# The sweep's convolution as two column tiles of 64 output rows, with the padding columns left out

## The chip, the cores and the metric

One NeuronCore of one Trainium2 chip, one launch. The metric is the device time of the launch in microseconds (us), the median of several runs. All data are float32.

## What is computed

The input x has shape (4, 64, 128, 128): 4 images, 64 channels, 128 rows, 128 columns. Four blocks follow each other, each as x = x + block(groupnorm(x)). Blocks 1 and 4 are pointwise networks over the 64 channels (block 4 with an attention over 8 heads). Blocks 2 and 3, each with four directional sweeps, hold the change. Cut to what matters, one sweep is

```python
def sweep(x, w, b, axis, reverse):        # w: 64 x 64 channels x 9 taps
    rows = moveaxis(x, axis, 0)           # 128 rows (or columns) of (4, 64, 128)
    if reverse: rows = rows[::-1]
    def step(prev, row):
        new = row + relu(conv1d(prev, w, padding=4) + b)
        return new, new                   # the next step needs this one
    _, rest = scan(step, rows[0], rows[1:])
```

So a sweep has 127 steps that depend on each other, and there are eight sweeps: down, up, right and left in block 2 (with bias), and the same four in block 3 (without). Each step is a convolution over 128 positions with 9 taps and 64 channels in and out, for 4 images. Positions outside the row count as zero.

## The kernel before, in words

**Layout.** The whole state stays on the chip. The 128 partitions hold 64 channels twice: partition q\*64 + channel holds the positions of parity q. A row of 128 positions is then 64 columns on 128 partitions, and the 9 taps over positions become 5 taps over columns (`TAPS2 = 5`) with 128x128 weight matrices `w_taps[:, n % 2, s, :]`, in which both parities in and out are mixed. `load_taps` fills the four 64x64 quadrants of each; a quadrant whose tap lies outside the nine stays zero. Columns 0 to 63 of a weight matrix make the outputs of parity 0, columns 64 to 127 those of parity 1.

**Two chains.** The four images are split into two chains c = 0, 1 of two images each. A chain's current row is in `x_row[c][par]`, of two images by 68 columns (`PADDED = HALF + 4`): 64 columns with two zero columns on either side, which GpSimd zeroes once at the start and nobody writes later. `par` alternates between steps.

**TensorE.** `conv` (L647 to L655) is one step of one chain: wait for `row_ready[c]` (L651), then five matmuls (L652 to L654) that accumulate in one PSUM bank. Each has a 128x128 weight matrix and streams 2 x 64 columns of `x_row`, shifted by s. The last raises `conv_done[c]`. `sweep` (L657 to L666) issues the convolutions of chain 0 and chain 1 in turn, in a hardware loop with four convolutions per round (two steps of two chains). The profile shows every float32 matmul as two LDWEIGHTS records and two MATMUL records, so one convolution is 10 of each, and the kernel has 8 x 127 x 2 = 2032 convolutions.

**VectorE.** `step` in VectorE's `sweep` waits for `conv_done[c]` and for ScalarE's `biased_row`, then L896 writes the new row into `x_row[c][par]` as max(conv, -bias) + (row + bias), which raises `row_ready[c]`. A second instruction or two (L899, L905) write the same values into the state, or in the upward sweeps into `turn_ring`. The first row of a forward sweep is a copy at L887.

**ScalarE** prepares `biased_row` ahead of the step (L454, L458). **SyncE** carries rows of the turned layout back (L274) in the upward sweeps, and loads and stores the residual of the block. While chain 0's new row is made, TensorE works on chain 1, and the other way round. The order of the instructions on each engine is written out in the program and held together by semaphores alone.

Outside the sweeps, `ffn` (L620, L624) streams 512 columns per matmul, the products of block 4 stream 256 (L704) and 128 columns (L715), `keep_warm` (L603) issues products that nobody reads, and a few small products stream 64 columns or 4 (L687, L690, L746).

Of the kernel before, what the change touches and what calls it, by code (L numbers as in the profile page):

```python
# [6 lines left out]
def build_program(nc, D, out):  # L7
# [20 lines left out]
    B, C, H, W = 4, 64, 128, 128  # L28
    P = 2 * C
    HALF = W // 2  # L30
    ROW = B * HALF
    PAIRS = H // 2
    TAPS2 = 5
    PADDED = HALF + 4
    CR = 8
    CHUNKS = H // CR
    NT = CR * HALF
    WH = HALF // 2
# [22 lines left out]
    with ctx:  # L61
        def sb(name, shape, dt=F32):
            return ctx.enter_context(nc.sbuf_tensor(name, shape, dt))
# [8 lines left out]
        res = sb("res", [P, RING_ROWS, B, WH])  # L72
        x_row = [[sb(f"x_row{c}{k}", [P, 2, PADDED]) for k in range(2)] for c in range(2)]
        biased_row = sb("biased_row", [P, 2, B, HALF])
        turn_ring = sb("turn_ring", [P, 2, 2, 2, B, WH])
        w_taps = sb("w_taps", [P, 2, TAPS2, P])
# [137 lines left out]
        def tile_of(j, b):  # L214

            return half_rows[:, bass.ts(j, 2 * CR), b, :]

# [20 lines left out]
        def slot(n, k):  # L238

            return (k + 1) % 2 if sweeps[n][2] else k  # L240
# [3 lines left out]
        def _(sp):  # L244
            for j in range(CHUNKS):
                sp.dma_start(state[:, j * CR:(j + 1) * CR, :, :, :].rearrange("p r g b w -> p r (g b w)"),  # L246
                             D["x"][:, j * CR:(j + 1) * CR, :]).then_inc(x_loaded[j], 16)

            def store_residual_a(j):

                for q in range(2):
                    for r in range(2):
                        src = state[q * C:(q + 1) * C, :, :, :, :].rearrange(
                            "c (j hp r) g b w -> c j hp r (g b w)", r=2, hp=CR // 2)[:, j, :, r, :]
                        dst = resid.rearrange("(j hp) (r c) s n -> j r c s hp n", hp=CR // 2, r=2)[j, r, :, q, :, :]
# [336 lines left out]
        def _(pe):  # L592
# [54 lines left out]
            def conv(n, c, k, hcount):  # L647

                par, src = slot(n, k), slot(n, 1 - k)
                out_ps = bank[2 * c + par][:, 0:2 * HALF].rearrange("p (b w) -> p b w", b=2)  # L650
                pe.wait_ge(row_ready[c], hcount)  # L651
                for s in range(TAPS2):  # L652
                    last = nc.tensor.matmul(out_ps, w_taps[:, n % 2, s, :], x_row[c][src][:, :, s:s + HALF],  # L653
                                            start=s == 0, stop=s == TAPS2 - 1)  # L654
                last.then_inc(conv_done[c], 1)  # L655

            def sweep(n):  # L657
                rev = sweeps[n][2]
                before = hbase(n) + (0 if rev else 1)
                pe.wait_ge(taps_loaded[n % 2], 64 * (n // 2 + 1))  # L660
                for c in range(2):
                    conv(n, c, 1, before)
                with pe.Fori(1, PAIRS) as i:
                    for k in range(2):
                        for c in range(2):
                            conv(n, c, k, i * 2 + (before + k - 1))  # L666
# [73 lines left out]
            for b in range(B):  # L740
                at = b // 2 * BANK + b % 2 * (P + 1)
                last = nc.tensor.matmul(pair[0][:, at:at + P + 1], gram_sb[:, b, :], q_ext[:, b, :], start=True, stop=True)
            last.then_inc(small_product_done, 1)
            operands()
            for b in range(B):
                nc.tensor.matmul(bank[2][:, b * C:(b + 1) * C], r_sb[:, b, 0:P], v_o1[:, 0, :], start=True, stop=True)  # L746
            nc.tensor.matmul(bank[3][:, 0:B], v_o1[:].rearrange("p r n -> p (r n)"), r_sb[:, :, P], start=False,
                             stop=True).then_inc(small_product_done, 1)
# [357 lines left out]
```

## Time and profile before

| | us |
|---|---|
| median of 3 runs (2888.72 to 2890.2) | 2889.41 |
| span of the profiled execution, first to last instruction | 2889.1 |
| TensorE, matmuls busy | 2749.3 (95%) |
| of these the sweep's convolution, L653 | 2276.2 |
| VectorE busy | 1905.5 (66%) |
| ScalarE busy | 1356.1 (47%) |
| mean granted TensorE clock over the span | 0.983 of 2.4 GHz |

The span is the time that the profile covers; it is 0.3 us under the median, so sums made on the span can be set beside the median as they are. A record's duration is not its cost: matmuls are pipelined, and the duration of one (274 ns at L653) covers more than two starts of the following ones. What a matmul costs in a stream is the distance from one start to the next. Times in the rows below are in us with two decimals; in a merged line the second number runs from the first start to the last end, "x" is the count, and the bracket is idle time before it and what ended it. PE is TensorE's matmul, PEld its weight load.

### The profile page before, as it was taken

To read this page: it belongs to the slowest core of one execution; us is meant where nothing else is said; L and a number is where in the kernel's file an instruction comes from. 1 tells how busy PE (TensorE), PEld (TensorE's weight loads), DVE (VectorE), ACT (ScalarE), POOL (GpSimd) and SP (SyncE) were. 2 spreads that over 40 slices of the span, in tenths; PEclk is the share of its full clock that TensorE was granted. 3 is DMA by queue.
4 is the path that set the end of the run, shared out by engine and by line. 5 is a ranking of instruction groups with operands and counts; after the bars stand their busy time and mean duration, and the time that the engine had idled before them with its cause. 6 is when DMAs were issued, how large, how long until landed. Compare 5 with 4: busy or idle time off the path is not lost.

```text
span 2889.1 us, 71107 instructions
## 1 busy us (share of the span) xinstructions
PE 2749.3 (95%) x22166; PEld 2581.7 (89%) x22166; DVE 1905.5 (66%) x6167; ACT 1356.1 (47%) x2660; POOL 66.4 (2%) x145
## 2 busy tenths in 40 slices
PE   2999999999999999996999999999999999879999
PEld 1369999999999999995999999999999999869943
DVE  7766666666666666677666666666666667779943
ACT  1766664222233333456666522223333335589978
POOL 0000000000000000000000000000000000013300
PEclk9999999999999999997999999999999999989999
DMA  6530001222300000026700022222000002210023
GB/s 246 143 92 0 0 0 26 59 59 59 95 0 0 0 4 0 0 73 186 268 0 0 4 58 58 58 66 54 0 0 0 0 0 57 74 44 0 0 87 145
DMA packets 158384, 145.83 MB, mean 50 GB/s; under 512 B 22738, under 2 KB 146068, under 8 KB 154260
## 3 DMA queue, kind: packets, MB, share of 16 engines
q1 hardware_dynamic: 146432, 142.65, 16.8%
q10 hardware_dynamic: 11924, 2.90, 0.5%
q14 instruction: 21, 0.17, 0.0%
q8 instruction: 7, 0.11, 0.0%
HBM read 61.61 MB, written 50.33 MB: 39 GB/s over the span
## 4 chain that ended last, share of the span: by engine, by line
PE 94%; DMA 2%; DVE 1%; SPq 1%; issue 1%; ACT 1%; ACTq 0%; DVEq 0%; POOLq 0%; POOL 0%
PE banks L653 78%; PE banks L624 4%; PE banks L620 4%; PE banks L704 4%; PE banks L715 2%; DMA state<-x_in 1%; PE banks L701 1%; SPq L246 1%; DMA res<-resid 1%; DVE state L973 0%; PE banks L603 0%; DMA resid<-state 0%; ACTq L402 0%; DMA state<-resid 0%; ACT banks L538 0%
## 5 line engine op out<-in xcount | busy, mean ns | idle before, releaser
L653 PE MATMUL banks<-x_row,w_taps 128*128 128x128 f32 x20320 | 2276.2, 274 | 10.8 <-DVE x_row L896 6.8
L653 PEld LDWEIGHTS banks<-x_row,w_taps 128*128 128x128 f32 x20320 | 2274.7, 191 | 12.5 <-DVE x_row L896 7.8
L896 DVE SCALAR_TENSOR_TENSOR x_row<-banks,sweep_nbias,biased_row 128x128 f32<-128x128 f32 x2032 | 713.2, 351 | 798.5 <-PE banks L653 783.1
L458 ACT ACTIVATE biased_row<-state,sweep_bias 128x256 f32 (+1 forms) x762 | 506.3, 665 | 1082.7 <-DVE state L899 628.2
L454 ACT ACTIVATE biased_row<-state,aff,gn_a 128x64 f32 (+1 forms) x1016 | 364.3, 430 | 202.1 <-DVE state L905 202.1
L899 DVE SCALAR_TENSOR_TENSOR state<-banks,sweep_nbias,biased_row 128x128 f32 (+1 forms) x1016 | 438.7, 432 | 0.2 <-issue 0.2
L905 DVE SCALAR_TENSOR_TENSOR turn_ring<-banks,sweep_nbias,biased_row 128x64 f32<-128x64 f32 x1016 | 237.3, 275 | 0.0
L905 DVE SCALAR_TENSOR_TENSOR state<-banks,sweep_nbias,biased_row 128x64 f32 (+1 forms) x1016 | 236.7, 274 | 0.1
L865 DVE TENSOR_TENSOR state<-banks,state 128x512 f32 x128 | 88.2, 689 | 100.1 <-PE banks L624 100.1
L624 PE MATMUL banks<-hid,ffn_w 128*128 128x512 f32 x256 | 134.6, 618 | 0.0
L704 PE MATMUL banks<-kv_w,res 128*128 128x256 f32 x512 | 131.5, 379 | 0.0
L620 PE MATMUL banks<-state,ffn_s 128*128 (+1 forms) x256 | 128.1, 603 | 0.3 <-DVE ffn_s L1053 0.3
L624 PEld LDWEIGHTS banks<-hid,ffn_w 128*128 128x128 f32 x256 | 43.6, 190 | 81.1 <-ACT hid L421 29.1
L704 PEld LDWEIGHTS banks<-kv_w,res 128*128 128x128 f32 x512 | 97.6, 191 | 13.6
L421 ACT ACTIVATE hid<-banks,ffn_b 128x512 f32<-128x512 f32 x128 | 87.5, 684 | 44.6 <-PE banks L620 43.4
L362 POOL TENSOR_TENSOR res<-res,ones 128x64 f32<-128x64 f32 x64 | 44.9, 702 | 2687.5 <-DVE res L1022 2687.5
L598 PE MATMUL banks<-mv,gmats 128*128 128x4 f32 x8 | 2.3, 361 | 109.0 <-DVE mv L780 56.0
L620 PEld LDWEIGHTS banks<-state,ffn_s 128*128 128x128 f32 x256 | 49.4, 194 | 61.8 <-issue 61.2
L423 ACT ACTIVATE state<-state,cb,a x128 | 102.7, 802 | 0.0
L598 PEld LDWEIGHTS banks<-mv,gmats 128*128 128x128 f32 x8 | 2.0, 311 | 110.2 <-DVE mv L790 53.4
L1007 DVE TENSOR_REDUCE res<-res 128x128 f32<-128x1024 f32 x64 | 78.1, 1220 | 18.1 <-ACT res L561 11.6
L522 ACT ACTIVATE banks<-state,minus_shift 128x256 f32 (+1 forms) x128 | 59.3, 463 | 57.3 <-DVE state L941 57.3
(115 smaller groups left out, 948.1 us busy)
## 6 DMA issues: line engine op xcount, KB each, us to landing
state<-turn_ring SPq DMA_DIRECT2D x512, 64.0 KB, 1.9
state<-x_in SPq DMA_DIRECT2D x16, 1024.0 KB, 20.9
resid<-state SPq DMA_DIRECT2D x64, 256.0 KB, 3.7
res<-resid SPq DMA_DIRECT2D x16, 1024.0 KB, 8.7
res<-resid SPq DMA_DIRECT2D x32, 512.0 KB, 5.3
resid<-state SPq DMA_DIRECT2D x16, 1024.0 KB, 11.1
out_y<-state SPq DMA_DIRECT2D x16, 1024.0 KB, 3.9
state<-resid SPq DMA_DIRECT2D x32, 256.0 KB, 9.3
```

The source lines that it names most:

```text
L421: nc.scalar.activation(hid[:, b % 2, :], bank[b % 2], func, bias=ffn1_b[:, b:b + 1]).then_inc(hidden_ready, 1)
L423: nc.scalar.activation(xs, xs, ACT.Identity, scale=a1[:, b:b + 1], bias=cb[:, b:b + 1]).then_inc(x_scaled, 1)
L454: last = nc.scalar.activation(biased_row[:, k, b, :].rearrange("p (g w) -> p g w", g=2), src, ACT.Identity, scale=gn_a[:, b:b + 1], bias=a ...
L458: nc.scalar.activation(as_cells(n, biased_row[:, k, :, :]), cells(n, slice(0, B), i, k, g), ACT.Identity, bias=sweep_bias[:, n:n + 1]).the ...
L620: nc.tensor.matmul(bank[b % 2], ffn1_s[:, b, :], tile_of(j, b), start=True, stop=True).then_inc(ffn_up_done, 1)
L624: nc.tensor.matmul(bank[2 + b % 2], ffn2_w[:, layer, :], hid[:, b % 2, :], start=True, stop=True).then_inc(ffn_down_done, 1)
L653: last = nc.tensor.matmul(out_ps, w_taps[:, n % 2, s, :], x_row[c][src][:, :, s:s + HALF], start=s == 0, stop=s == TAPS2 - 1)
L704: last = nc.tensor.matmul(ps[:, t * 2 * P:(t + 1) * 2 * P], y_st[:, k, col:col + P], kv_w[:], start=False, stop=t == 1)
L865: nc.vector.tensor_tensor(xs, bank[2 + b % 2].rearrange("p (r w) -> p r w", w=WH), xs, ALU.add).then_inc(ffn_added, 1)
L896: nc.vector.scalar_tensor_tensor(x_row[c][par][:, :, 2:2 + HALF], ps, nb, br, ALU.max, ALU.add).then_inc(row_ready[c], 1)
L899: last = nc.vector.scalar_tensor_tensor(cells(n, slice(2 * c, 2 * c + 2), i, k, g), ps, nb, br, ALU.max, ALU.add)
L905: last = nc.vector.scalar_tensor_tensor(new, ps[:, b, :].rearrange("p (g w) -> p g w", g=2), nb, br[:, b, :].rearrange("p (g w) -> p g w", ...
```

## The change

`conv` alone changes, with two constants. The five taps are taken in the order 2, 1, 3, 0, 4. Each tap's product is issued as two: the weight columns 0 to 63 into PSUM partitions 0 to 63, and the weight columns 64 to 127 into PSUM partitions 64 to 127. Both stream the same columns of `x_row`. Of these, the ones that lie in the zero padding are left out, with the output columns to which they add zero: tap 2 still covers all 64 columns of an image, taps 1 and 3 cover 63, taps 0 and 4 cover 62. Tap 2 comes first because the first product of an accumulation has to write every output column. The contraction stays at 128 partitions.

```diff
+    EDGE = 2
+    TAP_ORDER = (2, 1, 3, 0, 4)
...
                 pe.wait_ge(row_ready[c], hcount)
-                for s in range(TAPS2):
-                    last = nc.tensor.matmul(out_ps, w_taps[:, n % 2, s, :], x_row[c][src][:, :, s:s + HALF],
-                                            start=s == 0, stop=s == TAPS2 - 1)
+                for at, s in enumerate(TAP_ORDER):
+                    lo, hi = max(0, EDGE - s), min(HALF, HALF + EDGE - s)
+                    for q in range(2):
+                        blk = slice(q * C, (q + 1) * C)
+                        last = nc.tensor.matmul(out_ps[blk, :, lo:hi], w_taps[:, n % 2, s, blk], x_row[c][src][:, :, s + lo:s + hi],
+                                                start=at == 0, stop=at == TAPS2 - 1)
                 last.then_inc(conv_done[c], 1)
```

The waits and the semaphores are the same. A convolution has 10 matmuls in place of 5, so 20 LDWEIGHTS and 20 MATMUL records in place of 10 and 10, each load with 64 weight columns in place of 128.

## Rows read from the trace of the kernel before

**Rows 1.** The page's chain of work that ended last, by engine and line.
```profile
## 4 chain that ended last, share of the span: by engine, by line
PE 94%; DMA 2%; DVE 1%; SPq 1%; issue 1%; ACT 1%; ACTq 0%; DVEq 0%; POOLq 0%; POOL 0%
```

**Rows 2.** Groups of instructions, whole span: busy us, mean ns | idle before, releaser.
```profile
L653 PE MATMUL banks<-x_row,w_taps 128*128 128x128 f32 x20320 | 2276.2, 274 | 10.8 <-DVE x_row L896 6.8
L653 PEld LDWEIGHTS banks<-x_row,w_taps 128*128 128x128 f32 x20320 | 2274.7, 191 | 12.5 <-DVE x_row L896 7.8
L896 DVE SCALAR_TENSOR_TENSOR x_row<-banks,sweep_nbias,biased_row 128x128 f32<-128x128 f32 x2032 | 713.2, 351 | 798.5 <-PE banks L653 783.1
```

**Rows 3.** Busy time by engine in the first sweep, with granted clock.
```profile
core 0: us, PE busy (x) PEld busy (x) DVE busy (x) ACT busy (x) POOL busy (x), PEclk, DMA share, GB/s
188.24:471.80 283.56, 283.53 (x2539) 283.56 (x2540) 185.57 (x760) 181.60 (x507) 0.00 (x0) 1.00 0.00 0
```

**Rows 4.** Timeline of one stretch of the third sweep, all engines.
```profile
900.65 2.06 PE L653 MATMUL banks<-x_row,w_taps 128*128 128x128 f32 x17
900.76 1.87 PEld L653 LDWEIGHTS banks<-x_row,w_taps 128*128 128x128 f32 x16
900.94 0.35 DVE L896 SCALAR_TENSOR_TENSOR x_row<-banks,sweep_nbias,biased_row 128x128 f32<-128x128 f32 x1 [0.50 <-PE banks L653]
901.21 0.43 DVE L899 SCALAR_TENSOR_TENSOR state<-banks,sweep_nbias,biased_row 128x128 f32 x1
901.97 0.35 DVE L896 SCALAR_TENSOR_TENSOR x_row<-banks,sweep_nbias,biased_row 128x128 f32<-128x128 f32 x1 [0.33 <-PE banks L653]
```

**Rows 5.** Timeline of TensorE, matmuls of 512 columns in the last block.
```profile
2832.43 1.88 PE L620 MATMUL banks<-state,ffn_s 128*128 x4
2832.44 0.19 PEld L620 LDWEIGHTS banks<-state,ffn_s 128*128 128x128 f32 x1 [0.24 <-issue]
2832.86 0.19 PEld L620 LDWEIGHTS banks<-state,ffn_s 128*128 128x128 f32 x1 [0.24 <-issue]
```

**Rows 6.** Groups by form: the 512-column matmul's mean duration.
```profile
L620 PE MATMUL banks<-state,ffn_s 128*128 x240 | 117.7, 592 | 0.0
```

**Rows 7.** Timeline: loads of 64 and of 128 weight columns, at half the clock.
```profile
2549.20 0.29 PEld L687 LDWEIGHTS banks<-gn_c,wq_t 64*64 64x64 f32 x2 [2.19 <-DVE o_a L999]
2549.89 0.50 PEld L690 LDWEIGHTS banks<-q_col,uv 64*128 64x128 f32 x2 [0.40 <-DVE q_col L1001]
```

**Rows 8.** Timeline: products of 129 and of 64 columns, at half the clock.
```profile
2757.18 2.09 PE L742 MATMUL banks<-q_ext,res 128*128 128x129 f32 x8 [0.46 <-DVE res L1045]
2760.05 1.97 PE L746 MATMUL banks<-v_o,res 128*128 128x64 f32 x8 [0.79 <-DVE res L1047]
```

**Rows 9.** Timeline at the start of the second sweep, where TensorE had waited.
```profile
475.83 0.35 DVE L896 SCALAR_TENSOR_TENSOR x_row<-banks,sweep_nbias,biased_row 128x128 f32<-128x128 f32 x1 [2.91 <-ACT biased_row L458]
476.23 0.71 PE L653 MATMUL banks<-x_row,w_taps 128*128 128x128 f32 x4 [1.86 <-DVE x_row L896]
```

**Rows 10.** What ended TensorE's idle time before its convolutions: us, times.
```profile
L653 PE MATMUL banks<-x_row,w_taps x20320: 271/273/582, 188.3 to 2518.2; 128*128 128x128 f32 x200
  DVE x_row L896: 14.6, 10
  issue: 4.7, 3
```

## Prediction

> **What bounds the kernel now.** I read the chain of waits first: 94% of it is TensorE [rows 1]. The groups of instructions then name the line: the sweep's convolution, L653, has 2276 us of matmul records and only 10.8 us of idle time before them, while VectorE's L896 sat idle for 783 us waiting for those matmuls [rows 2]. So nobody keeps TensorE waiting; the time is what TensorE needs from one matmul start to the next. The first sweep gives it: 2540 loads in 283.56 us at a granted clock of 1.00 (2.4 GHz), 111.64 ns each [rows 3]. A convolution is 10 of these, 1116.4 ns, and 2032 convolutions make 2268.5 us of the span of 2889.1.
>
> What is in the 111.64 ns? Two things could set it, the stream of 128 columns or the load of 128 weight columns. **The stream:** four 512-column matmuls take 1.88 us from first start to last end, one lasts 0.592, so they start every (1.88 - 0.592) / 3 = 429.3 ns [rows 5, 6]. The load beside them takes 0.19 us and starts within 0.01 us of the matmul before, so here the stream is the bound: 512 columns at two cycles of 2.4 GHz are 426.7 ns, and 2.7 ns lie on top. For 128 columns this gives 106.7 + 2.7 = 109.4 ns. **The load:** at half the clock two loads of 64 columns take 0.29 us and two of 128 take 0.50, so 64 columns more cost (0.50 - 0.29) / 2 = 105 ns, again two cycles per column [rows 7]. 128 weight columns at full clock are thus 106.7 ns, 64 are 53.3. That a load can be the bound shows at half the clock too: 64 streamed columns behind a full load take 1.97 us for eight, hardly less than 129 columns with 2.09 [rows 8]. In the sweep both come to 106.7 ns, and the 2.2 ns that 111.6 has over the stream's 109.4 I read as the handover in a load-bound chain: a load starts just behind the start of the matmul before it, and the next matmul when it is in.
>
> **The change part by part.** Removed: nothing but columns. The five taps stream 128 + 2 x 126 + 2 x 124 = 628 columns in place of 640. By the stream's price the five taps are 628 x 2 / 2.4 + 5 x 2.7 = 536.8 ns per record, 1073.7 ns for the two records of a convolution. If a load of 128 columns still stood beside each, this would be worth nothing, since the load's 106.7 ns would go on setting the distance.
>
> Added: twice the records, each with half the weight columns. What that costs hangs on whether the two column tiles work side by side, and no row of before shows two tiles. From below: each tile has to stream all its columns itself, in two records per tap; if the other tile's run fully beside it, a convolution is 1073.7 ns, 42.7 less than now, x 2032 = -87 us. From above: the tiles take turns for the whole stream, and a convolution is 20 streams, 2147.4 ns, +1031.0, x 2032 = +2095 us. I take the neighbourhood of the lower end. The two tiles share no weight and no PSUM partition, and the rows show a load and a matmul of one array side by side already [rows 5], though not two matmuls.
>
> Between the ends stands the order of the records: the two of tile 0, then the two of tile 1. If matmuls start in that order, tile 1's first follows tile 0's second by a handover, then a stream passes until tile 1's second, and tile 0's next tap follows that by another. So each tap costs two streams and two handovers, and at 2.2 ns per handover a convolution is 1073.7 + 10 x 2.2 = 1095.7 ns: 20.7 ns less than now, x 2032 = **-42 us**. This is the sum that I forecast: 2889.1 - 42 = 2847, and as the span stands 0.3 us under the median, 2847 as a median as well. The loads have room in it: 4 x 53.3 = 213 ns per tap against 219 even if all went through one port, none if each tile had its own.
>
> The Trainium skill (TensorE: Matmul & The Clock Gate, Part 3, on the speedup of packing against the span model) puts about 4 ns between the starts of neighbouring tiles. With that in place of the 2.2 the convolution would be 1113.7 ns and the time 5 us below the present, about 2884. No run here shows two tiles, so the sum goes by the row.
>
> Costed at nothing, with their cover: **VectorE's reply.** It begins 0.27 us after the last matmul's start, takes 0.35, and TensorE starts 0.05 us after its end (475.83 + 0.35 to 476.23) [rows 2, 9], together 0.71 us with the gaps of 0.04. The other chain's convolution covers it, with 1.12 us plus the last record's own 0.11 now and 1.10 + 0.06 then; the cover shrinks from 0.52 to about 0.45 us. It would be gone only with convolutions under about 0.65 us. VectorE is busy for 185.6 of 283.6 us and ScalarE for 181.6 in the first sweep [rows 3], which becomes 67% and 65%. **The sequencer** has twice the records. TensorE's idle time put down to issue is 4.7 us, three times [rows 10], and the loop's own register steps don't show in the 111.64 ns. Doubled this is 5 us at most, which the range takes. **Odd starts** in PSUM and in `x_row` for the short taps: the old stream began at odd columns too for two taps of five, at no visible price; bound, the 12 columns saved, 20 ns per convolution, which would bring the gain to 1 us.
>
> **The rivals.** First, **the loads queue at one weight port**, and this one ends on the slower side. The place: tile 1's load can't begin before tile 0's second load is through, and that begins behind the start of tile 0's first matmul. Half a tap is then 53.3 + 53.3 + 2.7 and two or three handovers of 2.2 in a row, 113.7 to 115.9; a convolution of 1137 to 1159, up to 1164 if all 20 loads are strictly chained at 58.2 each. That is +42 to +97 us, and if the port hides its handovers, the present time. It decides as soon as a half tap of loads exceeds 111.6 ns. For it: the sweep is load-bound by my reading, and the count of loads' columns doesn't fall. Against: with loads that start ahead the handovers fall away. I take 2937 as its centre.
>
> Second, **records strictly in order, load and matmul alike**: tile 1's load waits until tile 0's second matmul has started, a full 53.3 + 2.7 + 2.2 = 58.2 ns lie open at each change of tile. A convolution is 1073.7 + 10 x 58.2 = 1655.7 ns, +539.3, x 2032 = +1096, so 3985 us. The rows can't refute it, since a load just behind the preceding matmul's start [rows 4, 5] is what a strict order would also show. The Trainium skill (same page, Part 3, what overlaps and what doesn't) lets a load overlap a running matmul only where the row groups differ, and column tiles share all rows; this rival is what that rule would do to the change of tiles. The trace already disagrees in part: L620's load lies wholly inside a running matmul of the same rows.
>
> Third, **the change doesn't do what it says**: the tiles take turns. That is the upper end from above, 4984 us. For it, only that no row shows two matmuls at once.
>
> **How the numbers follow.** A measurement of this kernel tells about 0.2%, 5.8 us, from no change. Separate tiles with small handovers: 0.49, nearly all of it faster (0.47), with 2802 and, by the bound for the odd starts, 2888 as ends. Loads at one port: 0.31, of which 0.07 falls within 5.8 us and 0.24 above. Strict order: 0.11. Turns: 0.09. Faster is 0.47, same 0.02 + 0.07 = 0.09, slower 0.24 + 0.11 + 0.09 = 0.44. The first two cases hold 0.80, so the range is theirs: from 2802, less 7 because the 2.7 comes from rows rounded to a hundredth, 2795, to 2889 + 97 + 5 for the issue, rounded to 2992. As both signs hold much of the chance, the likeliest case's own range is 2802 to 2888.
>
> **What would show it.** Right: a sweep's 5080 matmul records in about 278.5 us (54.8 ns each) at a clock of 1.00, tile 1's first matmul within some ns of tile 0's second, L896 still waiting for TensorE. A sweep of 284 to 296 us with even distances near 57 ns is the load port. Distances of 109 and 58 ns in turn are the strict order, 107 throughout the turns. What would make the forecast wrong altogether is a clock that falls in the sweeps, or VectorE becoming the releaser of TensorE's waits at L653.

## The result and the profile after

The changed kernel takes 2815.98 us (median; 2813.47 to 2816.73) against 2889.54 us in the same comparison: a ratio of 0.9744, 95% interval 0.9732 to 0.9755. That is 73.6 us less, on the forecast side and inside the range of 2795 to 2992, but 31 us below the forecast of 2847. The profiled execution's span fell from 2889.1 to 2814.8 us, by 74.3.

The page of the changed kernel, its groups of instructions (busy us, mean ns | idle before, releaser), beside [rows 2]:

```profile
L658 PE MATMUL banks<-x_row,w_taps 128*64 128x124 f32 (+2 forms) x40640 | 2201.7, 270 | 11.1 <-DVE x_row L901 6.8
L658 PEld LDWEIGHTS banks<-x_row,w_taps 128*64 128x64 f32 x40640 | 2199.5, 135 | 13.2 <-DVE x_row L901 8.2
L901 DVE SCALAR_TENSOR_TENSOR x_row<-banks,sweep_nbias,biased_row 128x128 f32<-128x128 f32 x2032 | 713.3, 351 | 718.9 <-PE banks L658 705.7
```

There are twice the records, and their busy time is 74.5 us less. A load lasts 135 ns where it lasted 191: 56 less, as the 64 weight columns fewer at two cycles of 2.4 GHz (53) let one expect. A matmul record still lasts 270 where it lasted 274, yet twice as many fit into less time, so they overlap. VectorE still waits for TensorE (705.7 us, 783.1 before), and TensorE's own idle time is unchanged at 11 us. The bound is where it was and has become cheaper.

The first sweep of the changed kernel, busy time by engine, beside [rows 3]:

```profile
188.47:462.72 274.25, 274.25 (x5082) 274.25 (x5082) 185.78 (x759) 181.86 (x507) 0.00 (x0) 1.00 0.00 0
```

The clock is 1.00 in both. From the first matmul of one convolution to the first of the next it is now 1080.0 ns where it was 1116.7: this is the steady distance, which the traces show in the second half of six of the eight sweeps. 36.7 ns x 2032 = 74.5 us is the whole difference of the spans (74.3). Nothing outside the sweeps pays or gains.

The single records show how the two tiles share TensorE. Here are starts in us around the border of two convolutions of the changed kernel (third sweep), read record by record from the trace, with the columns that each streams per image:

```
start    record  columns
900.216  matmul  62
900.256  matmul  62      last of the convolution, raises the semaphore
900.322  matmul  64
900.362  matmul  64
900.432  matmul  64
900.472  matmul  64
900.542  matmul  63
900.582  matmul  63
900.650  matmul  63
900.690  matmul  63
```

Each load begins 1 to 2 ns after the matmul record before it. The records come in pairs, 40 ns apart here, 20 in one sweep and 10 in five others, and what repeats is the pair: 110, 110, 108 ns. The trace doesn't name a record's tile. But where one tile works alone (below), its records start 105 to 111 ns apart, so the two of a pair belong to different tiles: two matmuls of over 105 ns of stream each run side by side. The offset between them costs nothing, since a convolution takes 1080 ns with each of the three.

### The profile page after: what moved, and what is told of

The parts are those of the page before. It is cut to its first block, busy times and chain, and to the rows that moved or that the text cites. A ratio compares the mean times of both kernels' runs of the same rounds, so it can differ in the third digit from the quotient of the medians.

```text
span 2814.8 us, 111747 instructions
## 1 busy us (share of the span) xinstructions
PE 2674.4 (95%) x42486; PEld 2506.7 (89%) x42486; DVE 1911.0 (68%) x6167; ACT 1361.5 (48%) x2660; POOL 66.4 (2%) x145
## 4 chain that ended last, share of the span: by engine, by line
PE 94%; DMA 2%; DVE 1%; SPq 1%; issue 1%; ACT 1%; ACTq 0%; DVEq 0%; POOL 0%; POOLq 0%
PE banks L658 78%; PE banks L626 4%; PE banks L622 4%; PE banks L709 4%; PE banks L720 2%; DMA state<-x_in 1%; PE banks L706 1%; DMA res<-resid 1%; SPq L248 1%; DVE state L978 0%; PE banks L605 0%; DMA resid<-state 0%; ACTq L404 0%; DMA state<-resid 0%; ACT banks L540 0%
## 5 line engine op out<-in xcount | busy, mean ns | idle before, releaser
L658 PE MATMUL banks<-x_row,w_taps 128*64 128x124 f32 (+2 forms) x40640 | 2201.7, 270 | 11.1 <-DVE x_row L901 6.8
L658 PEld LDWEIGHTS banks<-x_row,w_taps 128*64 128x64 f32 x40640 | 2199.5, 135 | 13.2 <-DVE x_row L901 8.2
L901 DVE SCALAR_TENSOR_TENSOR x_row<-banks,sweep_nbias,biased_row 128x128 f32<-128x128 f32 x2032 | 713.3, 351 | 718.9 <-PE banks L658 705.7
```

Source lines behind the costliest of these rows:

```text
L658: last = nc.tensor.matmul(out_ps[blk, :, lo:hi], w_taps[:, n % 2, s, blk], x_row[c][src][:, :, s + lo:s + hi], start=at == 0, stop=at == T ...
L901: nc.vector.scalar_tensor_tensor(x_row[c][par][:, :, 2:2 + HALF], ps, nb, br, ALU.max, ALU.add).then_inc(row_ready[c], 1)
```

## Experiments

All edits are to `conv` of the changed kernel. The time of a convolution is the steady distance from one convolution to the next; its change times 2032 gives the change of the whole within a few us.

### Columns left out, whole matmuls

```diff
-                    for q in range(2):
-                        blk = slice(q * C, (q + 1) * C)
-                        last = nc.tensor.matmul(out_ps[blk, :, lo:hi], w_taps[:, n % 2, s, blk], ...
+                    last = nc.tensor.matmul(out_ps[:, :, lo:hi], w_taps[:, n % 2, s, :], ...
```

> The padding columns left out and the tap order of the changed kernel, but whole 128x128 matmuls. If the kernel before was bound by the load of 128 weight columns (my reading of 111.6 ns per record), leaving columns out changes next to nothing: a convolution stays at 1110 to 1117 ns, 2877 to 2889 us. If the stream set the distance already before, the 12 columns of 640 are worth at least 20 ns per convolution (2848 us), and all 36.7 ns of the change (2816 us) if the column tiles bring nothing of their own.

Measured: 2889.85 us, ratio 1.0002 (0.9993 to 1.0011). The first sweep:

```profile
188.64:472.31 283.67, 283.67 (x2541) 283.67 (x2541) 185.99 (x759) 181.55 (x507) 0.00 (x0) 1.00 0.00 0
```

The steady distance is 1116.7 ns per convolution, 111.7 per record, as before, with 12 of 640 columns gone. By itself this half of the change is worth nothing, and the stream did not bind before.

### Two tiles, no column left out

```diff
-                    lo, hi = max(0, EDGE - s), min(HALF, HALF + EDGE - s)
+                    lo, hi = 0, HALF
```

> The two column tiles, but with all 64 columns of an image in every tap, padding included. By the load-bound reading the tiles free the stream from the load, and ten pairs of 110.7 ns (the distance of the 64-column pairs in the changed kernel) make 1107 ns: -10 ns x 2032, 2869 us. By the rival, that only the columns count, 2889 us, no change. If the tiles carried the whole gain, 2816 us.

Measured: 2846.97 us, ratio 0.9854 (0.9839 to 0.9869).

```profile
188.38:466.63 278.25, 278.25 (x5081) 278.25 (x5083) 185.83 (x759) 181.60 (x507) 0.00 (x0) 1.00 0.00 0
```

A convolution takes 1095 ns, not the 1107 of my expectation: a pair of 64-column records takes 109.5 on the mean. So the tiles alone bring 41.5 us, and the left-out columns bring the other 31 us only once the tiles are there. The two halves of the change do not add up from their single effects (0 and 41.5 against 73.6); the second needs the first.

### One tile nearly alone

```diff
-                    for q in range(2):
+                    for q in range(2 if at == 0 else 1):
...
-                                                start=at == 0, stop=at == TAPS2 - 1)
+                                                start=at == 0, stop=q == 1 or at == TAPS2 - 1)
```

The products of output channels of parity 1 for four of the five taps are left out.

> The changed kernel with tile 1's products of taps 1, 3, 0 and 4 left out: tile 0 does its ten records, tile 1 only two. If the tiles run fully beside each other and tile 0's own stream sets the time, a convolution stays near 1080 ns (1074 to 1080), 2803 to 2816 us. If tile 1 costs a start or a handover of its own, each of its eight missing records gives back its 2 to 4 ns: 1048 to 1064 ns, 2751 to 2783 us. If the tiles took turns in any part, far less still.

Measured: 2814.26 us, ratio 0.974 (0.9725 to 0.9755), the changed kernel's time.

```profile
L658 PE MATMUL banks<-x_row,w_taps 128*64 128x124 f32 (+2 forms) x24384 | 2201.3, 274 | 11.5 <-DVE x_row L901 7.3
L658 PEld LDWEIGHTS banks<-x_row,w_taps 128*64 128x64 f32 x24384 | 2199.1, 135 | 13.6 <-DVE x_row L901 8.6
188.76:462.51 273.75, 273.75 (x3051) 273.75 (x3048) 185.88 (x760) 181.35 (x506) 0.00 (x0) 1.00 0.00 0
```

16256 matmul records fewer, and the busy time is 2201.3 us in place of 2201.7. A convolution takes 1078.3 ns against 1080.0. So the second tile's eight records cost 1.7 ns together. This settles the forecast's two open prices: the handover between tiles (2.2 ns each, 22 ns in all) doesn't exist at a size that counts, and loads queueing at one port don't set the time of the changed kernel, since eight loads of 53.3 ns fewer would then have shown. One tile's own ten streams set the time.

### All taps of tile 0, then all of tile 1

```diff
-                for at, s in enumerate(TAP_ORDER):
-                    lo, hi = max(0, EDGE - s), min(HALF, HALF + EDGE - s)
-                    for q in range(2):
-                        blk = slice(q * C, (q + 1) * C)
+                for q in range(2):
+                    blk = slice(q * C, (q + 1) * C)
+                    for at, s in enumerate(TAP_ORDER):
+                        lo, hi = max(0, EDGE - s), min(HALF, HALF + EDGE - s)
```

> The same ten matmuls as in the changed kernel, all five taps of tile 0 first, then all five of tile 1. If each tile has its own queue of some depth, the time is the changed kernel's, 2816 us. If TensorE looks only one or two instructions ahead for work of the other tile, tile 0's ten records run alone but for the ends, then tile 1's: up to 2 x 1074 less the overlap at the border of two convolutions, 1700 to 2150 ns each, 4000 to 4990 us.

Measured: 3528.72 us, ratio 1.2216 (1.2198 to 1.2235): between the two expectations.

```profile
187.03:551.76 364.73, 364.53 (x5076) 364.48 (x5076) 185.99 (x761) 182.06 (x508) 0.00 (x0) 1.00 0.00 0
```

The same ten matmuls take 1432 ns per convolution in the steady stretches. Record by record, around the border of two convolutions of the second sweep:

```
start    record  columns
900.777  matmul  62      tile 1, tap 0, first record
900.781  load            tile 0 of the next convolution, carries its wait
900.783  matmul  64      tile 0, lasts 323 ns where the others last 267 to 272
900.882  matmul  62      tile 1, tap 0, second
900.946  matmul  64      tile 0
900.987  matmul  62      tile 1, tap 4, first
901.093  matmul  62      tile 1, tap 4, second, raises the semaphore
```

Tile 0's next work starts at the moment when tile 1's last matmul but one begins, with four records of tile 1 still to stream. A rule that fits: matmuls are handed out in program order, a tile holds one running and one waiting, and a third for the same tile holds up all that stand behind it. Then each half of a convolution is 6 streams to that point, 658 ns by the pair distances of the changed kernel below, and the tile's first load stands open, 323 - 270 = 53 ns: 711, measured 716.

### Taps in groups of two and of four

```diff
-                for at, s in enumerate(TAP_ORDER):
-                    lo, hi = max(0, EDGE - s), min(HALF, HALF + EDGE - s)
-                    for q in range(2):
+                for group in ((0, 1), (2, 3), (4,)):
+                    for q in range(2):
                         blk = slice(q * C, (q + 1) * C)
+                        for at in group:
...
```

The run with groups of four has `((0, 1, 2, 3), (4,))` there.

> The changed kernel's ten matmuls, two taps of tile 0, then two of tile 1, and so on. In the run with all taps of tile 0 first, a half of a convolution took 716 ns where a tile's ten streams need 1078: 362 ns, 3.4 records, of the other tile ran beside it. If that is a fixed lookahead of about 3.4 records, groups of four records leave 0.6 of one (some 65 ns) uncovered at four of the borders between groups: 1080 to 1350 ns per convolution, 2816 to 3370 us, with 2950 as a middle. If any departure from strict alternation loses all overlap, 4 of 5 taps run one tile at a time: near 1900 ns, above 4400 us.

Measured: 2817.62 us, ratio 0.9748 (0.9733 to 0.9763), 1080 ns per convolution, the lower end of what I expected. Strict alternation isn't needed.

> Four taps of tile 0, four of tile 1, then the fifth of each. Theory A, formed on the run with all five taps of a tile first: matmuls are issued in program order, and a tile holds one running and one waiting; the next one for the same tile blocks all behind it until the waiting one starts. Then tile 1 begins when tile 0's third tap does, and in groups of four neither tile runs dry: 1080 ns per convolution, up to 1190 if each switch exposes half a load as it does with groups of five; 2816 to 3040 us. Theory B, a fixed lookahead of 3.4 records, leaves 4.6 of 8 records uncovered at two borders of a convolution: some 1080 + 2 x 4.6 x 54 = 1580 ns, 3830 us.

Measured: 3084.53 us, ratio 1.0681 (1.0664 to 1.0697), a convolution of 1213 ns. Both expectations miss, the one with the rule by 44 us, the fixed lookahead by 745. The rule gives most of it if carried through: tile 1's first load stands open for 53 ns, this delays its third tap, behind which tile 0's fifth waits, and that one's load stands open as well, 106 of the 133 ns. The other 27 stay open. That the rule is the chip's own is not shown: it fits the orders in ones, in twos and in fives, and four fifths of what the fours cost.

### Four column tiles

```diff
-                    for q in range(2):
-                        blk = slice(q * C, (q + 1) * C)
+                    for q in range(4):
+                        blk = slice(q * C // 2, (q + 1) * C // 2)
```

> Four column tiles of 32 outputs, same columns streamed, four matmuls per tap. If lookahead and starts allow it, each tile's own ten streams set the time as with two tiles: 1078 to 1090 ns, 2812 to 2836 us. With a lookahead of 3.4 records (1.7 matmuls) no more than two or three tiles can be busy at once, since a tile's next tap stands four matmuls behind: at two tiles busy a convolution is 20 streams, 2157 ns, 5000 us; at three 1438 ns, 3540 us.

Measured: 2826.2 us, ratio 0.978 (0.9765 to 0.9795).

```profile
L658 PE MATMUL banks<-x_row,w_taps 128*32 128x124 f32 (+2 forms) x81280 | 2205.4, 270 | 16.8 <-DVE x_row L901 8.7
188.94:463.70 274.76, 274.76 (x10162) 274.75 (x10163) 185.94 (x759) 181.84 (x507) 0.00 (x0) 1.00 0.00 0
```

40 matmul records per convolution, one every 27 ns, take the time of 20, as in the first of the two expectations. Of the 10 us that the whole is slower, 5.7 are TensorE's idle time before the convolutions (16.8 against 11.1). Smaller tiles bring nothing, since each still streams every column, and the issue of records isn't near its limit with two tiles.

### Taps 1 and 3 with 62 columns

Tap 1 writes columns 2 to 63 and tap 3 columns 0 to 61 of each image in the first run, both 1 to 62 in the second, so a few edge columns lack a tap's product.

```diff
-                    lo, hi = max(0, EDGE - s), min(HALF, HALF + EDGE - s)
+                    lo, hi = {0: (2, 64), 1: (2, 64), 2: (0, 64), 3: (0, 62), 4: (0, 62)}[s]
...
+                    lo, hi = {0: (2, 64), 1: (1, 63), 2: (0, 64), 3: (1, 63), 4: (0, 62)}[s]
```

> The changed kernel with taps 1 and 3 cut from 63 to 62 columns per image, so that two edge columns lack one tap each: a price of the odd count, not a version to use. By columns alone the four pairs of records give back 1.67 ns each, 6.7 ns per convolution: 13.5 us, 2802. If the 63-column records cost 109.5 ns because of the odd count or the odd start, and 62-column ones cost 105.2 as in taps 0 and 4, it is 4 x 4.3 = 17 ns: 35 us, 2781.

Measured: 2817.54 us, ratio 0.9753 (0.974 to 0.9766): no gain at all from four columns less per convolution, so neither expectation came in.

> Taps 1 and 3 with 62 columns per image as in the earlier run that gained nothing, but now the streamed columns start at an even one (2 and 4, where they started at 3) and the output at an odd one (1). Each of the two taps lacks one more edge column. If the odd start of the stream cost the 4 ns, the four pairs fall to 105 ns and a convolution to about 1063, 2781 us. If the odd start of the output costs the same, or neither does, 2816 us as before.

Measured: 2789.49 us, ratio 0.965 (0.9637 to 0.9663), 26.5 us below the changed kernel and 8 above the expectation for a price of the odd stream start. The distances from pair to pair, means over 100 convolutions of the first sweep, in ns, two pairs per tap:

```
                          tap 2         tap 1         tap 3         tap 0         tap 4        sum
64 columns everywhere   111.3 109.4   109.6 109.4   111.1 109.7   108.8 108.0   108.2 109.6   1095
changed kernel          110.5 109.6   108.8 109.8   110.9 108.6   105.0 105.0   106.0 105.8   1080
62, stream from odd     111.1 109.4   107.4 109.9   110.3 109.8   105.1 104.9   106.2 105.9   1080
62, stream from even    110.9 109.6   105.0 105.1   105.9 105.8   105.8 105.8   105.8 105.8   1066
```

An even count read from an even column of `x_row` takes 105 to 106 ns. With the count odd (tap 1 of the changed kernel, from column 2) or the first column odd (62 from column 3), it takes 107 to 111, nearly what 64 columns take. With 64 columns the first one makes no such difference: taps 1 and 3, from an odd column, take 109.4 to 111.1, the others 108.0 to 111.3. The odd start of the output costs nothing. So of the change's 12 columns, the 8 of taps 0 and 4 bring 13 of the 15 ns, the 4 of taps 1 and 3 two. The faster kernel leaves products out; a complete one needs 63 columns in these taps, and I have none that gets them from even reads.

### Whole matmuls with half the stream

```diff
-                    lo, hi = max(0, EDGE - s), min(HALF, HALF + EDGE - s)
-                    for q in range(2):
...
+                    lo, hi = 0, HALF if at == 0 else HALF // 2
+                    last = nc.tensor.matmul(out_ps[:, :, lo:hi], w_taps[:, n % 2, s, :], ...
```

> Whole 128x128 matmuls as in the kernel before, but taps 1, 3, 0 and 4 stream only the first 32 of an image's 64 columns, so most of the output lacks four taps: 384 of 640 columns are left. If the load of 128 weight columns binds, the distance stays at 111.7 ns for all ten records and the time at 2889 us. If the stream binds, eight records take 56 ns: a convolution of 667 ns, which is below what VectorE's reply lets through (some 760), so about 2150 to 2200 us.

Measured: 3910.3 us, ratio 1.3534 (1.3509 to 1.3559), over 1000 us more than either expectation. The five executions took between 3908.71 and 4169.11 us; the profiled one has a span of 4166.9. Its first and its third sweep:

```profile
187.47:729.20 541.73, 541.73 (x2540) 541.73 (x2541) 185.84 (x759) 181.47 (x507) 0.00 (x0) 0.50 0.00 0
1277.46:1561.10 283.64, 283.64 (x2541) 283.64 (x2542) 176.29 (x506) 93.60 (x127) 0.00 (x0) 1.00 0.06 15
```

In the third sweep the clock is 1.00 and 2540 loads take 283.6 us, 111.67 ns each: with 64 columns streamed in place of 128 in eight records of ten, the distance hasn't moved. That is the load bound, shown where the clock is the same. In the first sweep the granted clock is 0.50, and 213.3 ns per record are 128 weight columns at two cycles of 1.2 GHz. This execution had five of its eight sweeps at the lower level, 213.3 ns per record in each. The granted clock fell at 182.4 us, just behind a pause of TensorE from 177.3 to 181.5. In the kernel before it fell at the same pause (178.3 to 182.5), at 181.3, but there it was back at 1.00 at 188.2, where the sweep begins. Here it came back only at 1274.7, although TensorE was busy for all of the first sweep's 541.73 us. Why it stayed down isn't shown.

## Why the prediction was right, and where it was off

**The bound before: right.** The load of 128 weight columns set the distance of 111.64 ns, and leaving columns out alone changed nothing (ratio 1.0002); halving the stream in eight records of ten left it at 111.67.

**The stream's price: 4.6 ns too low.** I had 1073.7 ns for a convolution's ten streams; one tile nearly alone takes 1078.3. The step at fault is the even price of 2 / 2.4 ns for each column: the 63-column records of the changed kernel take 109.5 ns where I had 107.7, which is 7.3 ns for a tile's four. The others nearly cancel: 110.05 for 109.4 at 64 columns, 105.5 for 106.0 at 62. "Odd starts", with a bound of 20 ns, were the right place to look. My reason for putting them at nothing was wrong, though: the old stream began at odd columns "at no visible price" because the load set its distance, so no price of the stream could be seen there.

**The handover between tiles: the term that was mis-sized.** I took 10 x 2.2 ns, on the ground that tile 1's first record starts behind tile 0's second. The second tile costs 1.7 ns per convolution in all, and the records of the tiles alternate instead of following in program order. This is what the 31 us consist of: 20.3 ns too much for the second tile less 4.6 too little for the stream are 15.7 ns (1095.7 - 1080.0), x 2032 = 32 us. That the two errors have opposite signs is luck. The lower end from below, 1073.7 ns and 2802 us, was the better model with the odd columns added.

The sum assumed that the 2.2 ns come back on top of every record's stream. But 111.67 ns is the distance behind a full load with 64 streamed columns as with 128, and 109.5 ns is the distance of a stream of 2 x 64 columns once the tiles are there: the 2.2 are the difference of two prices, one of the load and one of the stream, and no handover that a stream pays. With 64 weight columns a load is 53 ns under a stream of 105 and no longer the bound.

**One weight port: refuted as priced.** The tile that ran nearly alone had eight loads fewer and saved 1.7 ns, where the rival had a convolution at 1137 to 1164 ns. The trace of the changed kernel points the same way: where the loads of a pair start 10 ns apart, each lasts 134 to 136 ns, as where they start 40 apart, though one takes 53 by its columns.

**Strict order: refuted for this kernel** (1080.0 ns against 1655.7), **but not empty.** Order matters, as 1432 ns with all taps of a tile in a row show. The kernel's alternation, and groups of two just as well, keep clear of it. The Trainium skill (TensorE: Matmul & The Clock Gate, Part 3, what overlaps and what doesn't) has loads overlap a running matmul only where row groups differ, and matmuls start and end strictly in program order. The trace disagrees on the overlap and on the order of starts, for column tiles of equal rows: in the changed kernel each load starts while matmuls of both tiles run, and with tile by tile tile 0's next product starts at 900.783 while three records of older ones start at 900.882, 900.987 and 901.093.

**Turns: refuted** (1080.0 ns against 2147.4). **The covers held:** VectorE waited for TensorE for 705.7 us, and TensorE's idle time stayed at 11 us with twice the records.

## What to carry to other kernels

Here 128 weight columns and 128 streamed ones both come to 106.7 ns, and the load was the bound, at 111.67 ns against the stream's 109.5. So compare what 64 and 128 streamed columns cost behind a full load before leaving columns out. Two column tiles of half the weights freed the stream from the load for 1.7 ns in 1080, as long as at most two matmuls in a row went to the same tile; rows of four and five lost part of the overlap, and three were not run. After that columns count, but here only in even counts from even columns.

## What the runs showed of the hardware that I had not expected

- Matmuls of different column tiles start out of program order, but not without limit: 1080 ns per convolution in groups of one or two taps, 1213 in groups of four, 1432 in groups of five. In the last the other tile's work starts when one matmul of the first runs and one waits.
- A float32 stream of 63 columns per image, or of 62 from an odd column, costs nearly as much as one of 64: 107 to 111 ns against 105 to 106 for 62 from an even column.
- Less work per record can double the time. With the stream halved behind full loads, five of eight sweeps ran at a granted clock of 0.50, with 213 ns per record for 112, the first of them with TensorE busy throughout; the other three of the same execution ran at 1.00.
